# Expert outputs added in rounds of 2, 4, 2, and the attention projection as two products by head parity

## The reference

```python
x = x + deformable_conv(ln(x))           # 8 groups x 9 points, bilinear samples, projection
t = t + experts(ln(t))                   # layer 0
x = x + neighborhood_attention(ln(x))    # 8 heads of 16, window 7x7, projection
t = t + experts(ln(t))                   # layer 1

def experts(x):                          # 8 experts, 128 -> 512 -> 128, top 1
    probs = softmax(x @ gate_w + gate_b); idx = argmax(probs)
    kept = position_within_expert(idx) < C
    hmid = relu(x @ w1[e] + b1[e]); y = hmid @ w2[e] + b2[e]
    return nan_to_num(y[idx] * (prob * kept))
```

## Time and profile before

| | us |
|---|---|
| median of 3 runs (2549.48 to 2552.93) | 2552.23 |
| the profiled execution | 2552.92 |
| its span, first to last instruction | 2551.1 |
| TensorE busy with products | 2269.3 (89%) |
| VectorE busy | 1895.3 (74%) |
| GpSimd busy | 1668.8 (65%) |
| ScalarE busy | 1223.9 (48%) |
| mean granted TensorE clock | 0.965 |

### The profile page before, as it was taken

One profiled execution on the slowest core, in us unless ns is written; L12 is line 12 of the kernel. 1 busy time (PEld: TensorE's weight loads), 2 busy tenths in 40 slices (PEclk: granted clock), 3 DMA queues, 4 the chain that ended last, 5 costly groups with the idle time before them and its releaser, 6 DMA issues.

```text
span 2551.1 us, 61174 instructions
## 1 busy us (share of the span) xinstructions
PE 2269.3 (89%) x18976; PEld 2157.1 (85%) x18976; DVE 1895.3 (74%) x4404; ACT 1223.9 (48%) x3974; POOL 1668.8 (65%) x1797
## 2 busy tenths in 40 slices
PE   1487799999999999999999999999999999999887
PEld 1387698988988898898889898889999998999877
DVE  5576687777877777787777777877778878877543
ACT  1133354554554545455455455545554555455455
POOL 3777777777777776766666776767777777775000
PEclk6798899999999999999999999999999999999999
DMA  8522222222222222222122222212112111111000
GB/s 192 159 58 59 65 67 60 59 65 67 65 66 61 63 58 63 66 61 61 56 56 58 67 62 60 64 54 58 57 58 59 57 58 57 57 57 43 9 23 5
DMA packets 219754, 158.70 MB, mean 62 GB/s; under 512 B 149530, under 2 KB 186988, under 8 KB 219596
## 3 DMA queue, kind: packets, MB, share of 16 engines
q0 software_dynamic: 55296, 113.36, 14.9%
q1 hardware_dynamic: 164300, 43.73, 7.6%
HBM read 138.90 MB, written 18.04 MB: 62 GB/s over the span
## 4 chain that ended last, share of the span: by engine, by line
PE 56%; DVE 14%; issue 12%; ACT 8%; POOL 7%; DVEq 1%; SPq 1%; DMA 0%; ACTq 0%; POOLq 0%
PE Y L1598 14%; PE DGB L1496 12%; PE Z L1587 11%; POOL got L897 7%; PE DGB L1539 4%; DVE acc L1207 3%; ACT hid L1410 3%; ACT L1395 3%; PE N L1641 2%; PE N L1659 2%; PE N L1506 2%; DVE made L1059 2%; PE N L1546 2%; DVE turns L1277 1%; PE N L1667 1%
## 5 line engine op out<-in xcount | busy, mean ns | idle before, releaser
L897 POOL DMA_INDIRECT got<-patches,ranks x1728 | 1653.8, 957 | 639.3 <-issue 495.5
L1410 ACT ACTIVATE hid<-Z,b 128x128 f32<-128x128 f32 x2048 | 577.0, 372 | 501.0 <-PE Z L1587 499.5
L1059 DVE TENSOR_TENSOR made<-TW,tent 128x1152 f32<-128x1152 f32 x512 | 690.9, 1351 | 17.9 <-PE DGB L1496 14.4
L1496 PE MATMUL DGB<-ident,made 128*128 128x128 f32 x4608 | 596.4, 275 | 56.5 <-DVE bias L1125 41.2
L1598 PE MATMUL Y<-w,hid 128*128 128x128 f32 x4096 | 576.9, 284 | 68.4 <-DVE acc L1207 60.3
L1598 PEld LDWEIGHTS Y<-w,hid 128*128 128x128 f32 x4096 | 505.4, 194 | 109.9 <-DVE acc L1207 60.7
L1496 PEld LDWEIGHTS DGB<-ident,made 128*128 128x128 f32 x4608 | 523.1, 142 | 70.4 <-DVE bias L1125 42.0
L1587 PE MATMUL Z<-xt_m,w 128*128 128x128 f32 x4096 | 539.2, 278 | 0.5 <-ACT xt_m L1392 0.5
L1587 PEld LDWEIGHTS Z<-xt_m,w 128*128 128x128 f32 x4096 | 498.0, 194 | 6.9 <-issue 6.6
L1345 ACT ACTIVATE spread<-DGB 128x256 f32<-128x256 f32 x256 | 97.9, 382 | 389.4 <-PE DGB L1496 383.6
L1136 DVE TENSOR_TENSOR got<-got,TW 128x1152 f32<-128x1152 f32 x192 | 258.6, 1347 | 23.3 <-DMA got<-patches,ranks 22.1
(11 more groups left out here) (192 smaller groups left out, 2329.0 us busy)
## 6 DMA issues: line engine op xcount, KB each, us to landing
got<-patches,ranks POOLq DMA_INDIRECT x1728
vwin<-vpad SPq DMA_DIRECT2D x320, 40.0 KB
patches<-arena SPq DMA_DIRECT2D x92, 96.0 KB
w<-in_L_ffn_w SPq DMA_DIRECT2D x2, 2048.0 KB
patches<-got SPq DMA_DIRECT2D x38, 96.0 KB, 2.2
vpad<-vt SPq DMA_DIRECT2D x128, 16.0 KB
out<-X SPq DMA_DIRECT2D x32, 64.0 KB
X<-in_x SPq DMA_DIRECT2D x1, 576.0 KB, 4.4
```

The source lines that it names most:

```text
L897: pool.indirect_dma_start(out=got[:, q, j * PATCH:(j + 1) * PATCH], out_offset=None, in_=table, in_offset=bass.IndirectOffsetOnAxis(ap=ran ...
L1059: v.tensor_tensor(made[:, n % MADE, :].rearrange("p (k y x) -> p k y x", k=K, y=CHUNK), weighed.rearrange("p (k y) -> p k y", k=K)[:, :, c ...
L1410: ins = a.activation(hid[:, e % 2, c, :], Z[e % 2][:, c * P:(c + 1) * P], ACT.Relu, bias=b1[n][:, e * FC + c:e * FC + c + 1])
L1496: ins = pe.matmul(DGB[:, n % 2 * P:(n % 2 + 1) * P], made[:, n % MADE, k * P:(k + 1) * P], ident[:, :], is_transpose=True, start=(k == 0), ...
```

## The change

The expert outputs are added in rounds of 2, 4 and 2: experts 0 and 1 at the head of VectorE's step 4 (once y3 is there), 2 to 5 at the head of step 6 (once y5 is there), 6 and 7 in `close`. Down product 4 waits for a1, down product 6 for a5, down product 0 of the next half for a7 as before.

The attention output is copied so that a partition keeps only the columns of its own pair of heads (four copies of 32 partitions by 128 columns on each of the two engines, in place of one of 128 by 512), and the projection is two products, one with the rows of the even heads, one with those of the odd heads.

Other steps move within the slot. Second layer's half: `gate_T` of layer 1 from early in step 2 to late in step 2, behind down product 2; q/k/v turn from step 4 to 3, project from 5 to 4, parts from 6 to 5; `split` from 5 to 2; `corners` from 7 to 3; `gate_T` of layer 0 from early to late in step 7. First layer's half: the turn of layer 1's normed tile from ahead of flow 15 to behind it.

```diff
...
         base = sb("base", [P, B, DG])
         iota = sb("iota", [P, W])
-        heads = sb("heads", [P, NH])
+        heads = sb("heads", [P, NH + 2])
         dec = sb("dec", [P, E])
...
         bq = sb("bq", [P, 2])
         bv = sb("bv", [P, D])
-        wp = sb("wp", [P, NH, D])
+        wp = sb("wp", [P, 2, D])
         bias = sb("bias", [P, 3, 3, KK])
...
         qbd = turns[:, :].rearrange("p (j h q) -> p j h q", j=NB, h=NH)
         PT = turns[:, :].rearrange("p (j q) -> p j q", j=NB)
-        OT = turns[:, :].rearrange("p (h q) -> p h q", h=NH)
+        OT = turns[:, 0:2 * P].rearrange("p (r q) -> p r q", r=2)
         st_p = turns[:, 0:NT * 6].rearrange("p (t s) -> p t s", t=NT)
-        OT_of = OT.rearrange("p h (a k w) -> p (h a) k w", a=BLK, k=2)
+        OT_of = OT.rearrange("p r (a k w) -> p (r a) k w", a=BLK, k=2)
+        PAIR = 2 * HD
         vwin = sb("vwin", [P, NB, D])[:, :, :]
...
                         if e == 1 and e1:
                             route("count", 1, i - 4)
-                        if e == 2 and e1:
-                            route("gate_T", 1, i - 4)
                         if e == 3 and e1:
...
                         if e == 6 and ends:
                             route("count", 0, i - 1)
-                        if e == 7 and ends:
-                            route("gate_T", 0, i - 1)
                         return
...
                     if e == 2:
                         if e1:
+                            route("gate_T", 1, i - 4)
                             route("gated", 1, i - 4)
...
                             qkv("stats", i - 2, u0_before)
                             qkv("root", i - 2)
+                        if placed:
+                            places("split", i - 1 + PLEAD)
                     if e == 3:
...
                         if qk:
                             qkv("norm", i - 2)
+                            qkv("turn", i - 2)
                         if val:
                             values("norm", i + LEAD)
+                        if placed:
+                            places("corners", i - 1 + PLEAD)
                     if e == 4:
...
                             route("turned", 0, i - 1, u0_before)
                         if qk:
-                            qkv("turn", i - 2)
+                            qkv("project", i - 2)
                     if e == 5:
-                        if qk:
-                            qkv("project", i - 2)
                         if ends:
                             route("pick", 0, i - 1)
-                        if placed:
-                            places("split", i - 1 + PLEAD)
+                        if qk:
+                            qkv("parts", i - 2)
                     if e == 6:
                         if ends:
                             route("exp", 0, i - 1)
-                        if qk:
-                            qkv("parts", i - 2)
                     if e == 7:
                         if ends:
+                            route("gate_T", 0, i - 1)
                             route("gated", 0, i - 1)
-                        if placed:
-                            places("corners", i - 1 + PLEAD)
                         if place:
...
                         if att:
                             route("norm", 1, i - 3)
-                            route("turn", 1, i - 3, None, None, i + PLEAD if place else last)
-                            route("turned", 1, i - 3, u1)
                     flow(8 + e)
+                    if e == 7 and att:
+                        route("turn", 1, i - 3, None, None, i + PLEAD if place else last)
+                        route("turned", 1, i - 3, u1)
                     if e == 1 and att:
...
             dense("make", 0, 0)
             v.wait_ge(const_in, CONSTS)
-            for h in range(NH - 1, -1, -1):
-
-                v.wait_ge(setup, 7 + (NH - 1 - h))
-                v.tensor_scalar(wp[:, h, :], wp[:, 0, :], heads[:, h:h + 1], None, ALU.mult).then_inc(setup, 1)
+            for odd in (1, 0):
+
+                v.wait_ge(setup, 7 + (1 - odd))
+                v.tensor_scalar(wp[:, odd, :], wp[:, 0, :], heads[:, NH + odd:NH + odd + 1], None, ALU.mult)\
+                    .then_inc(setup, 1)
             v.wait_ge(rpb_in, 16 * BLK * BLK)
             bt = bias[:, :, :, :].rearrange("p t j k -> p (t j) k")
             v.tensor_tensor(bt, bt, prob[:, 0:1, :].to_broadcast([P, 9, KK]), ALU.add).then_inc(setup, 1)
-            v.wait_ge(setup, 8 + NH)
+            v.wait_ge(setup, 8 + 2)
...
                     v.tensor_scalar(gate, kept, small[n][:, 4:5], None, ALU.mult).then_inc(*s("gate"))
-            def add_up(u, n, t, e0, e1):
+            def add_up(u, n, t, e0, e1, out):
...
                 gate = route_b[n][:, 5, :]
-                v.wait_ge(*exp_t.done(f"y{e1 - 1}", u))
+                v.wait_ge(*exp_t.done(f"y{out}", u))
                 for e in range(e0, e1):
...
                 for e in range(E):
                     if e == 4:
-                        add_up(u, n, t, 0, 4)
+                        add_up(u, n, t, 0, 2, 3)
+                    if e == 6:
+                        add_up(u, n, t, 2, 6, 5)
                     beside(e, True)
...
                 d, s = exp_v.done, exp_v.step
                 xt = X[:, bass.ds(t, 1), :].rearrange("p o d -> p (o d)")
-                add_up(u, n, t, 4, E)
+                add_up(u, n, t, 6, E, E - 1)
...
                 if part == "values":
                     v.wait_ge(*att_t.done("o", t))
-                    v.tensor_copy(OT_of[:, :, 1, :], N[1][:, :].rearrange("p (g w) -> p g w", g=NH * BLK)).then_inc(*s("o1"))
+                    for a in range(0, P, PAIR):
+                        at = a // HD * BLK * 16
+                        ins = v.tensor_copy(OT_of[a:a + PAIR, :, 1, :], N[1][a:a + PAIR, at:at + P]
+                                            .rearrange("p (g w) -> p g w", g=2 * BLK))
+                    ins.then_inc(*s("o1"))
                 if part == "add":
...
                 if part == "values":
                     a.wait_ge(*att_t.done("o", t))
-                    a.activation(OT_of[:, :, 0, :], N[0][:, :].rearrange("p (g w) -> p g w", g=NH * BLK), ACT.Copy)\
-                        .then_inc(*s("o0"))
+                    for c in range(0, P, PAIR):
+                        at = c // HD * BLK * 16
+                        ins = a.activation(OT_of[c:c + PAIR, :, 0, :], N[0][c:c + PAIR, at:at + P]
+                                           .rearrange("p (g w) -> p g w", g=2 * BLK), ACT.Copy)
+                    ins.then_inc(*s("o0"))
...
                         pe.wait_ge(*exp_v.done("a7", u - 1))
                     if e == 4:
-                        pe.wait_ge(*exp_v.done("a3", u))
+                        pe.wait_ge(*exp_v.done("a1", u))
+                    if e == 6:
+                        pe.wait_ge(*exp_v.done("a5", u))
                     for c in range(FC):
...
                     pe.wait_ge(*att_s.done("o0", t))
                     pe.matmul(N[0][:, 0:D], ones[0:1, :], rows[:, :], start=True, stop=False)
-                    for h in range(NH):
-                        ins = pe.matmul(N[0][:, 0:D], OT[:, h, :], wp[:, h, :], start=False, stop=(h == NH - 1))
+                    for odd in range(2):
+                        ins = pe.matmul(N[0][:, 0:D], OT[:, odd, :], wp[:, odd, :], start=False, stop=(odd == 1))
                     ins.then_inc(*s("proj"))
```

More of the change, by code:

```diff
@@ L1278, in attend @@
                                     .unsqueeze(2).to_broadcast([P, NB, NH, BLK * BLK]),
-                                    heads[:, :].unsqueeze(1).unsqueeze(3).to_broadcast([P, NB, NH, BLK * BLK]),
+                                    heads[:, 0:NH].unsqueeze(1).unsqueeze(3).to_broadcast([P, NB, NH, BLK * BLK]),
                                     ALU.mult).then_inc(*s("qbd"))
@@ L1528, in _ @@
                     places(part, t, (LEAD - 1, -1))
-            pe.wait_ge(setup, 8 + NH)
+            pe.wait_ge(setup, 8 + 2)
             def conv(part, t, q=None, mine=None):
@@ L1693, in constants @@
         "c_iota": np.broadcast_to(np.arange(W), (P, W)).astype(f),
-        "c_heads": (p[:, None] // HD == np.arange(NH)[None, :]).astype(f),
+        "c_heads": np.concatenate([p[:, None] // HD == np.arange(NH)[None, :],
+                                   p[:, None] // HD % 2 == np.arange(2)[None, :]], 1).astype(f),
         "c_dec": np.broadcast_to(np.arange(E, 0, -1).astype(f), (P, E)).copy(),
```

## The result

The changed kernel takes 2686.9 us (median of 4 runs, 2683.87 to 2687.26), the kernel before 2551.4 (four runs): ratio 1.0529, 95% interval 1.0511 to 1.0547. It is slower, as forecast, but by 135 us where 34 were forecast, and outside the range. The profiled execution has a span of 2682.1, 131.0 more than before.

A forecast was written before the change was run, and what follows sets the result against it. TensorE's order of work was taken to set the slot. Slots with values +17, without +24.5, slot 3 +1, slots 30 and 31 -1 each, tail -7: +33 on a 2551.1 us span, forecast 2586, range 2528 to 2618.

The forecast's parts named there:

- The term of the clock: Drops to 1.2 GHz at three in four of the new 4.2 us waits: 1.0 us per slot, bounds 0 and 1.7.
- The wait for a5: First layer's down product 6 waits while VectorE does copies, make, places, then adds: new 4.2 us per slot with places.
- The loop edge: VectorE waits 2.99, adds two, waits 1.56, adds two; the 1.56 was assumed to fall behind the two remaining adds.
- T0: Second layer's first down product, behind the loop edge: its 1.82 us wait was to go, with TensorE leading.
- The other waits: Per slot: 1.35 us at second layer's down product 4, 0.7 at its down product 6, 0.4 and 0.3 at gate turns.
- The projection: Eight products become two: 1.5 us less on TensorE per slot; smaller copies make VectorE 0.4 later, bounds 0 and 0.8.
- Slots 30, 31 and the tail: Without places, 1.2 us of the new wait is left: -1 each; tail -7 from three projections and shorter adds.
- B: Rival, faster: the 1.56 us edge wait is no longer met and the clock does not drop; 2529 us, chance 0.16.
- C: Rival, faster: all waits go and the slot falls to POOL's 69 us; 2415 us, chance 0.06.
- D: Rival, no change: stalls 1 us smaller than worked out, copies at 0, drops rare; 2553 us, chance 0.08.
- E: Rival, slower still: slots without values meet the edge's fetch waits, every stall drops the clock (0.7 more); 2618 us, chance 0.10.
- T4: Second layer's fifth down product (down product 4): new wait of 1.35 us, as split and corners precede its adds.

The follow-up runs named there:

- wait_filled_n0: The changed kernel with 18 unread identity products issued ahead of the first layer's wait for a5: 2597.6 us, ratio 1.0184.
- only_rounds: The kernel before with the rounds of 2, 4, 2 alone, projection and all other steps as before: 2683.38 us, ratio 1.0508.
- moves_alone: The kernel before with the moved steps alone, projection and rounds as before: 2555.2 us, ratio 1.0009.
- projection_alone: The kernel before with the projection by head parity alone (two products, eight small copies, two masked matrices): 2550.84 us, ratio 0.9997.
- rounds_undone: The changed kernel with the rounds back at 4 and 4, projection and moves kept: 2567.33 us, ratio 1.0064.

## Why the prediction was right and wrong

**The size, by its terms.** The sum took 74.9 us for a slot with values and 74.8 for one without at full clock, and 1.0 more for the clock. `wait_filled_n0` shows the full-clock slots: 76.29 and 75.32. So the sum of work and waits along the two engines was 1.4 and 0.5 short. **The term of the clock is the step that failed:** 1.0 was taken, with 1.7 as the upper bound, and 3.36 and 3.06 were measured. Over the slots: clock 19 x 2.36 + 7 x 2.06 = 59 us, work and waits 19 x 1.4 + 7 x 0.5 = 30, start, tail and the slots around the loops some 9; with the 33 forecast on the span this is the 131.

Where the clock's number came from: I divided the tail's loss in one stretch by one wait (1.8 us beside a wait of 4.1 at most), then took three in four of them and called part of it absorbed. But the tail's stretch was at half rate for 3.4 us, and behind this wait the engine stays there for 6.8 us, in 6 of the 19 slots with values for 10.2; every slot has it; and little of it is absorbed, since TensorE leads there. In the slots with values the half rate adds up to 150 us, 7.9 per slot, which is 3.95 of lost work, and 3.36 came as time. The Trainium skill ("TensorE: Matmul & The Clock Gate", section "HAM oscillation") says that every turn of such a loop pays, and the trace agrees: 26 slots of 26. The price of 1.7 per slot that the prediction put beside it is the tail's, and it was half of what the slots with values took.

**The wait for a5** (forecast 4.2, measured 4.52; 3.7 in `only_rounds`, without the smaller copies): right in place and cause, and near in size. The copies took 1.22 between starts, where 1.05 was taken, and make and places 4.49, where 4.26 was.

**The loop edge.** I assumed that the wait of 1.56 would fall behind the two adds that are left, so that TensorE would lead. It came between them (3.19, then 2.14), ahead of a7, and T0 waited 0.8 to 1.1 us for a7, where no wait was forecast. This is most of the 1.4. The runs show what moved the wait: it stands ahead of a6 in the kernel before and in `moves_alone`, and ahead of a7 in `projection_alone` and `rounds_undone`, which keep all four adds, as in the changed kernel. So the projection's part moved it, by one add, and taking two adds out of `close` did not. The Trainium skill ("Runtime: NRT & Kernel Launch", section "Instruction fetch mechanics") says that a taken branch out of the fetched pages stalls. The traces agree as far as they go: instruction packets and the edge's waits are there together or missing together (no packets and 0.41 in `only_rounds`; also 0.4 in the slots without values of the changed kernel).

**The other waits** (forecast, then measured): down product 4 of the second layer 1.35, 0.74; its down product 6 0.7, 0.60; gate turns 0.4 and 0.3, none and 0.20. Not foreseen: 0.38 ahead of the first gathered sum, for a spread copy. Together the slot's idle time is 7.8 us, where 7.0 was worked out.

**The projection.** It saves 1.34 on TensorE, where 1.5 was taken; right that VectorE decides around the edge; alone it is worth nothing. Not foreseen: all kernels with it start the loop 3 to 5 us later. VectorE's wait for the loads in the setup is 26.2 us in `projection_alone`, against 21.0 in the row of that wait before; what in them is slower was not tried.

**Slots 30, 31 and the tail:** -9 forecast (-1 each and -7), -3.8 measured for all behind slot 29. The same stretch is 9.4 shorter in `projection_alone` and 4.9 longer in `only_rounds`, so the rounds seem to cost there, where they were taken to save a little. These are single executions, and no run was made for it.

**The rivals.** B (the edge pays) needed a clock that holds, and it fell in every slot; `only_rounds`, where the edge's waits are gone, is no faster. C fell by the wait for a5. D fell. E named the right kind, a stall that drops the clock in every slot, but its price of 0.7 more was too small, and the instruction fetch of the slots without values, its other half, did not come.

**What it said one would see:** accumulation over 150 us (195.7) and gate below 40 (17.8), single waits near 4.2: right. A wait of 1.3 at T4: there, but 0.74. Slots of 75 to 76: wrong.

## What to carry to other kernels

Ahead of giving a semaphore one more reader, ask what stands before the releasing instruction on its engine: one step of VectorE moved behind the adds (places) was worth 81 us. Price a standstill of TensorE twice: by its length, and by the slower products behind it, and take the second price from a row of the same kernel with the same standstill, or leave its bound wide. Where such a wait can't be removed, products into a free part of a bank keep the clock: they made the kernel before 0.6% faster (2538.51 us, ratio 0.9941) and the changed one 89 us.

## What the runs showed of the hardware

- Behind a standstill of 4.5 us TensorE ran at 1.2 GHz for some 7 us (granted clock 0.53 over 7.09 us), in all 26 slots of the two loops; with 4.0 of it filled, in none.
- Behind one of 2.5 us it ran at half rate in 12 of 19 slots with values and at full rate in the others, with the same work around it: some 79.4 or 76.3 us, no value between. Behind the 1.6 to 2.4 at the loop edge of the kernel before it did so in 11 of 19.
- VectorE's waits behind the loop edge (some 3 us, then 1.1 to 2.4) come with instruction packets, five per slot; in `only_rounds` and in slots without values the edge costs 0.4 us. The second wait stayed ahead of a7 when two adds ahead of it were taken out of `close`, and was longer by about 1 us (1.08 in `rounds_undone`, 2.14 in the changed kernel).
